# Last pass of a graph network: another row order, five chunks' layers from split parts, shorter split lead

## The reference

```python
def mlp(x, W1, b1, W2, b2, W3, b3):            # a = leaky_relu, slope 0.01
    return a(a(a(x @ W1 + b1) @ W2 + b2) @ W3 + b3)

x = layernorm(x + relu((adj @ x) @ kernel + bias))
u = x
for _ in range(3):
    v = mlp(adj @ u, *uv)
    u = mlp(adj @ v, *vu)                      # the third u is not used
out = layernorm(x + v)
```

## Time and profile before

| | |
|---|---|
| median of three runs | 1168.94 us (1168.66 to 1168.98) |
| the profiled execution | 1168.49 us |
| its span, first to last instruction | 1166.7 us, so 1.8 us lie around it |
| granted TensorE clock | 0.999 of full |
| TensorE busy, its weight loads | 99 %, 82 % |
| VectorE, ScalarE busy | 63 %, 57 % |

### The profile page before, as it was taken

The page is one execution under the profiler, slowest core; times in us unless marked ns, Lnnn a source line. Parts: engine busy times, 40 slices in busy tenths (PEclk is TensorE's granted clock), DMA queues, the critical chain, the costliest instruction groups (busy, mean ns, idle before and its releaser), DMA issues.

```text
span 1166.7 us, 13724 instructions
## 1 busy us (share of the span) xinstructions
PE 1153.5 (99%) x5242; PEld 954.0 (82%) x5242; DVE 736.7 (63%) x888; ACT 659.3 (57%) x811; POOL 4.9 (0%) x10
## 2 busy tenths in 40 slices
PE   7999999999999999999999999999999999999998
PEld 6888888888888888888888888888888888887876
DVE  7997676458555555555545746553566554678985
ACT  7765555346554555555444755553556544667874
POOL 0000000000000000000000000000000000000001
PEclk9999999999999999999999999999999999999999
DMA  9988786568356646555656636655575656579971
GB/s 383 405 301 322 251 270 198 200 216 288 120 205 217 210 157 213 199 195 181 205 188 220 238 124 211 205 179 198 192 242 165 212 186 230 166 292 356 312 281 36
DMA packets 72353, 261.60 MB, mean 224 GB/s; under 512 B 8032, under 2 KB 8800, under 8 KB 71264
## 3 DMA queue, kind: packets, MB, share of 16 engines
q1 hardware_dynamic: 72144, 260.61, 64.0%
q10 hardware_dynamic: 144, 0.13, 0.0%
HBM read 258.61 MB, written 2.10 MB: 223 GB/s over the span
## 4 chain that ended last, share of the span: by engine, by line
PE 94%; DMA 3%; DVE 1%; ACT 0%; SPq 0%; issue 0%; ACTq 0%
PE agg_ps L932 29%; PE agg_ps L925 28%; PE agg_ps L918 28%; PE pre_ps L829 4%; DMA adj_raw<-in_adj 3%; PE hid_ps L790 1%; PE hid_ps L792 1%; PE hid_ps L791 1%; DVE adj_lo L770 1%; PE hid_ps L851 1%; PE hid_ps L865 0%; ACT adj_hi L635 0%; DVE stats L648 0%; PE hid_ps L868 0%; SPq L496 0%
## 5 line engine op out<-in xcount | busy, mean ns | idle before, releaser
L770 DVE TENSOR_TENSOR adj_lo<-adj_raw,adj_hi 128x1024 fp32r<-128x1024 f32 x464 | 547.8, 1219 | 224.9 <-ACT adj_hi L635 219.6
L918 PE MATMUL agg_ps<-adj_hi,feat_hi 128*128 128x512 f32 x1484 | 586.4, 395 | 7.5 <-ACT adj_hi L635 7.5
L925 PE MATMUL agg_ps<-adj_hi,feat_lo 128*128 128x512 f32 x1484 | 579.3, 390 | 0.0
L635 ACT ACTIVATE adj_hi<-adj_raw 128x1024 fp32r<-128x1024 f32 x464 | 467.6, 1051 | 83.3 <-PE agg_ps L932 69.1
L932 PE MATMUL agg_ps<-adj_lo,feat_hi 128*128 128x512 f32 x1484 | 458.8, 390 | 0.2 <-DVE adj_lo L770 0.2
L918 PEld LDWEIGHTS agg_ps<-adj_hi,feat_hi 128*128 128x128 f32 x1484 | 279.6, 188 | 66.0 <-issue 9.4
L925 PEld LDWEIGHTS agg_ps<-adj_hi,feat_lo 128*128 128x128 f32 x1484 | 279.5, 188 | 59.1 <-issue 1.9
L932 PEld LDWEIGHTS agg_ps<-adj_lo,feat_hi 128*128 128x128 f32 x1484 | 278.9, 188 | 59.5 <-DVE adj_lo L770 1.1
L528 ACT ACTIVATE hid<-hid_ps,params 128x512 f32<-128x512 f32 (+2 forms) x82 | 55.1, 672 | 59.6 <-PE hid_ps L792 50.7
L600 ACT ACTIVATE in_hi<-part 128x512 fp32r<-128x512 f32 x24 | 15.2, 634 | 110.3 <-DVE part L759 110.3
L528 ACT ACTIVATE post<-pre 128x512 f32<-128x512 f32 x39 | 24.7, 632 | 88.0 <-DVE pre L737 88.0
(11 more groups left out here) (80 smaller groups left out, 389.8 us busy)
## 6 DMA issues: line engine op xcount, KB each, us to landing
adj_raw<-in_adj SPq DMA_DIRECT2D x472, 512.0 KB, 5.6
adj_raw<-in_adj SPq DMA_DIRECT2D x8, 1024.0 KB, 8.1
resid<-in_x SPq DMA_DIRECT2D x8, 256.0 KB, 8.1
out<-resid SPq DMA_DIRECT2D x7, 256.0 KB, 5.3
params<-in_weights SPq DMA_DIRECT2D x1, 386.0 KB, 5.1
b_row<-in_bias_rows SPq DMA_DIRECT2D x1, 128.0 KB, 5.7
out<-resid SPq DMA_DIRECT2D x2, 64.0 KB, 1.8
out<-resid ACTq DMA_DIRECT2D x1, 128.0 KB, 1.9
```

Of the source, the lines that this page charges most:

```text
L635: act.activation(split_hi(b)[:, i * CHUNK:(i + pieces) * CHUNK], adj_raw[:, h % RAW, 0:pieces * CHUNK], ACT.Copy).then_inc(adj_hi_ready, 1)
L770: dve.tensor_tensor(split_lo(b)[:, slot], adj_raw[:, h % RAW, 0:pieces * CHUNK], split_hi(b)[:, slot].bitcast(F32), ALU.subtract).then_inc ...
L918: pe.matmul(group_bank(g), feat_hi[feats][:, tile(src, i)], split_hi(b)[:, piece(i)], start=start, stop=False)
L925: pe.matmul(group_bank(g), feat_lo[feats][:, tile(src, i)], split_hi(b)[:, piece(i)], start=False, stop=False)
```

## The change

Three things change, all in the last pass. The row order becomes 6, 1, 5, 4, 3, 2 (after 7 and 0). The first five units (rows 0, 7, 6, 1, 5) become `LAST_PARTS`: they are calculated in parts like the units of the passes 1 to 4, with offsets of their own that reach to piece 36 after the row's end. Splits are due 14 pieces ahead, not 20. Row 4 takes the kind `LATE2` and row 3 the kind `LATE`, both with new offsets; the activation of `LATE2` goes to a buffer of its own (a part of `part` that is free by then), so it needn't wait until the unit before it is normalised.

```diff
-LEAD, FIRST_LEAD, LAST_LEAD, FIRST_ROWS = 12, 4, 20, 3
+LEAD, FIRST_LEAD, LAST_LEAD, FIRST_ROWS = 12, 4, 14, 3
...
+    LAST_PARTS: dict(dve_sum=0, act_in=3, dve_in=4, pe_hid1=10, act_hid1=11, dve_hid=13, pe_hid2=20, act_hid2=21,
+                     pe_out=25, dve_pre=25, act_post=28, dve_stats=29, act_std=32, dve_shift=33, act_norm=36),
...
-    LATE3: dict(dve_sum=0, act_in=0, pe_hid1=6, act_hid1=7, pe_hid2=10, act_hid2=11, pe_out=14, dve_pre=14,
-                act_post=16, dve_stats=17, act_std=20, dve_shift=20, act_norm=24),
-    LATE2: dict(dve_sum=0, act_in=1, pe_hid1=4, act_hid1=5, pe_hid2=7, act_hid2=8, pe_out=9, dve_pre=10,
-                act_post=10, dve_stats=12, act_std=14, dve_shift=15, act_norm=16),
-    LATE: dict(dve_sum=0, act_in=1, pe_hid1=1, act_hid1=2, pe_hid2=3, act_hid2=5, pe_out=5, dve_pre=7, act_post=7,
-               dve_front=8, dve_total=8, dve_stats=9, act_std=12, dve_root=13, pool_norm=13),
+    LATE2: dict(dve_sum=0, act_in=0, pe_hid1=5, act_hid1=6, pe_hid2=9, act_hid2=10, pe_out=13, dve_pre=13,
+                act_post=14, dve_stats=15, act_std=18, dve_shift=18, act_norm=22),
+    LATE: dict(dve_sum=0, act_in=1, pe_hid1=3, act_hid1=4, pe_hid2=5, act_hid2=7, pe_out=7, dve_pre=9, act_post=9,
+               dve_front=10, dve_total=10, dve_stats=11, act_std=14, dve_root=15, pool_norm=15),
...
-LAST_ROWS = (6, 5, 4, 3, 1, 2)
+LAST_IN_PARTS = 5
+LAST_ROWS = (6, 1, 5, 4, 3, 2)
...
-                          "act_post": max(ends.get("act_norm", -1) if self.steps_of(u) != END else -1,
+                          "act_post": max(ends.get("act_norm", -1) if self.steps_of(u) not in (LATE2, END) else -1,
...
-                else LATE3 if after == 3 else LAST
+                else LAST_PARTS if u < self.rows * (PASSES - 1) + LAST_IN_PARTS else LAST
...
-        return self.steps_of(u) in (IN_PARTS, TURN)
+        return self.steps_of(u) in (IN_PARTS, TURN, LAST_PARTS)
...
-            if plan.steps_of(u) in (END, END2):
+            if plan.steps_of(u) in (LATE2, END, END2):
                 return part_of(chunk_of(plan.first_of(u) - 1))
...
-                        wait_for_normed(act, u - 1)
+                        if plan.steps_of(u) != LATE2:
+                            wait_for_normed(act, u - 1)
...
-                u = at(t, "dve_hid", HIDDEN)
+                u = at(t, "dve_hid", DEEP)
...
-                u = at(t, "dve_in", HIDDEN)
+                u = at(t, "dve_in", DEEP)
```

More of the change, by code:

```diff
@@ L40 @@
 HOLD = 3
-LEAD, FIRST_LEAD, LAST_LEAD, FIRST_ROWS = 12, 4, 20, 3
+LEAD, FIRST_LEAD, LAST_LEAD, FIRST_ROWS = 12, 4, 14, 3
 LOAD_GCN, LOAD_PARAMS = 24, 90
 W_SPLIT = 320
-IN_PARTS, TURN, LATE3, LATE2, LATE, END, END2 = "in_parts", "turn", "late3", "late2", "late", "end", "end2"
+IN_PARTS, TURN, LAST_PARTS, LATE2, LATE, END, END2 = "in_parts", "turn", "last_parts", "late2", "late", "end", "end2"
 STEPS = {
```

## The result

| | before | changed |
|---|---|---|
| median of five runs | 1168.78 us (1168.54 to 1168.98) | 1175.79 us (1175.39 to 1177.12) |
| profiled execution | 1168.49 us, span 1166.7 | 1175.79 us, span 1174.0 |

The ratio is 1.0062, 95 % interval 1.0048 to 1.0076: slower, by 7.0 us. The lines of the changed file lie one or two further down: 528 and 560 are now 529 and 561, 918, 925, 932 are now 920, 927, 934; 790 is 792, 851 and 865 are 853 and 867, 829 is 831, 770 is 772, 759 is 761, 745 and 750 are 747 and 752, 737 is 739, 635 is 637.

What follows compares the result with a forecast made beforehand. TensorE, 99 % busy, was taken to set the time, with VectorE and ScalarE nearly full in the last pass. -1.8 + 9.2 - 0.2 = +7.2 us on 1168.5 gives 1175.7 profiled, 1176.1 median; range 1168.0 to 1179.0.

Steps and rivals of the forecast that it cites:

- the likeliest case: Last pass: TensorE waits 5 to 10 us for layers, giving 1172 to 1177.5 us; chance 0.62.
- TensorE's saving, 1.8 us: Five units, two layers each: a layer in parts takes 0.68 us, not 0.86, so 1.8 us less TensorE work.
- The added work: Last pass, units in parts: VectorE gets 6.0 us more work, ScalarE 4.4 us more.
- The waits, 9.2 us: TensorE at layers of rows 6, 1, 5 and 3, by a walk of the queues: 9.2 us, 0.26 there already.
- VectorE's idle times in the stretch, 8.1 us in 15: From row 7's dve_hid (piece -89) to row 3's sum (-12): VectorE loses 8.1 us, 14 waits for ScalarE splits.
- The written-out link: Row 1's statistics (-41) to row 5's second layer (-28): VectorE needs 7.2 us, starts 5.0 late, TensorE waits 2.7.
- The lead: Splits due 14 pieces ahead, not 20: doesn't cause the waits; with 20 the walk gives 3 us less.
- The loads: Each load is issued 8 splits, about 10.9 us, ahead of use and lands in 5.6 us: hidden.
- The tail: From piece -9 to the end: as long as before, what follows piece -3 being the same list.
- VectorE keeps up: Rival, last pass: every layer finds its parts, only saved work shows, -1.8 - 0.3, 1166.8 us; chance 0.15.
- Work alone: Rival: VectorE's 65.9 us without holes, only row 3's sum late, about 1168.0; half or no holes, chance 0.15.
- The clock falls: Third rival: TensorE's waits lower its clock, +2.5 us, 1178.6, or loads land late; chance 0.08 for clock or loads.

Runs made afterwards that it cites:

- the plan without waits: Changed kernel, all five units still in parts, with row order 1, 6, 5, 4, 3, 2, lead 17 and other offsets: 1166.25 us, ratio 0.9979 to the kernel before.
- the one with lead 20: Changed kernel with splits due 20 pieces ahead again, all else as changed: 1173.84 us, ratio 1.0041 to the kernel before.
- the later square root: Changed kernel with act_std, dve_shift and act_norm of the units in parts 2 pieces later, same work: 1172.34 us, ratio 1.0036 to the kernel before.
- the lighter ScalarE: Changed kernel normalising only the first of four tiles of a chunk in the five units in parts: 1173.54 us, ratio 1.0038 to the kernel before.
- the one with lead 24: Laid-out plan (row order 1, 6, 5, 4, 3, 2) with lead 24 in place of 17: 1175.36 us, ratio 1.0053 to the kernel before.
- the kernel with row 4's statistics behind the sum: Changed kernel with row 4's dve_stats, act_std and dve_shift 2 pieces later, behind row 3's sum on VectorE: 1173.41 us, ratio 1.0040 to the kernel before.

## Why the prediction was right

It said 1176.1 us and 1175.79 was measured, by the likeliest case and its mechanism. That the profiled execution agrees within 0.1 us (1175.7 was said for it) is partly luck: the waits came out 0.5 us smaller than said, and 0.7 us that the prediction didn't have makes up for them. Nor did the median lie 0.45 us above the profiled execution this time; it is the same. Point by point:

- *TensorE's saving, 1.8 us.* Not seen by itself in the changed kernel, but in the plan without waits: 2.4 us faster by the medians, where 1.8 and the 0.3 us wait of before make 2.1. In the sum of TensorE's work in the stretch two terms are 0.1 us too large (7 x 0.68 is 4.8 and 2 x 0.86 is 1.7), so 66.5 should be 66.3 us; the argument stays.
- *The added work.* VectorE's 6.0 us is what the page shows. Of ScalarE's 4.4 us it shows 3.4, as busy time; what the eight instructions cost in the queue wasn't measured apart.
- *The waits, 9.2 us* (the six that are listed make 9.1). From start to start on TensorE, less the normal distance: row 6's second layer 1.6 (1.5 was said), row 1's output layer 0.2 (0.4), row 5's first layer 1.2 (1.2) and second 2.6 (2.7), its output under 0.1 (0.2), row 3's first layer 3.1 (3.1). Together 8.7, of which 0.3 was there before; less the saved 1.8 that makes 6.6 us. The two traces move apart by 6.9 us in the last pass, so 0.3 has no name; the other 0.4 of the 7.3 us between the two profiled executions is there at the pass's beginning (an output layer at 1044.70, before at 1044.26).
- *VectorE's idle times in the stretch, 8.1 us in 15.* All waits of VectorE from 1083 to 1155 us in the changed kernel:

```profile
DVE adj_lo L772 <- ACT adj_hi L637: 3.7, 8, 0.9
DVE feat_lo L772 <- ACT feat_hi L637: 2.4, 6, 0.6
DVE part L720 <- ACT part L529: 0.7, 1, 0.7
```

  Fifteen, of 6.8 us: 14 for ScalarE's splits and one for row 4's activation, as said. The term was a little too large, as was the lateness: at row 1's statistics 6.0 us where the walk had 6.4. (They start at 1127.55. Their piece lies three pieces, 2.04 us, before the one at which row 5's first layer was due, 1123.11 + 0.45 = 1123.56.) VectorE doesn't once wait for TensorE at 739 there; such a wait was named as the sign of being wrong.
- *The written-out link.* From 1127.55 to the end of `hid_lo` at 1134.78: 7.2 us, with holes of 0.21 and 0.58 where 0.27 and 0.66 were said.
- *The lead.* It was said not to be the cause of the waits, and to give back 3 us at 20. Measured 2.0 by the medians, 3.4 by the profiled executions (the last section is on the difference).
- *The loads.* "Hidden" holds for TensorE, which waits for no split in the last pass. ScalarE did wait for them: seven times, 3.0 us in all, between 1054 and 1067 us, where the kernel before and the one with lead 20 have no such wait. They don't carry into the stretch: VectorE is idle 3.11 us after them, before 1071.87, and with lead 20, without them, the waits at rows 6 and 5 are the same.
- *The tail* is as long: from the last product (853, 256 columns) on both kernels are 7.3 us apart, as at the end.

The rivals. *VectorE keeps up*: it doesn't, at these offsets; the plan without waits shows that it can. The Trainium skill (Perfetto Trace Analysis, Identifying the Most-Contended Engine) says to optimise the engine with the highest occupancy first, over the span TensorE. The work saved there shows in these runs only where TensorE has no wait in the last pass. The section Optimization Strategy of the same page says that the most contended engine can change over time; the windows agree, with VectorE at 44.70 and TensorE at 45.06 of 50 us from 1100 on. *Work alone*: refuted twice, by the later square root and by the lighter ScalarE, 3.4 and 2.3 us less by the medians with VectorE's work unchanged. *The clock falls*: the profiled execution shows 0.999 for the span and 1.00 in each of the windows with waits, but other executions show something of it. The 5 us of slower products in its price stand in no row, and no run shows them.

## What to carry to other kernels

Where one engine is busy all the time and two others feed it from queues in order, the question is not how much work they have over the span but whether their queues, in the stretch at hand, still reset: here a VectorE that waited for TensorE at the output layers had spare time, and one that never did stayed late by the sum of all that came before. An instruction that waits for the other helper stood better behind the work that this one needs next. And before giving up a cheaper form because it came out slower, walk the queues with the durations of the trace: the same instructions cost 7 us in one order of rows and set of offsets and gave 2.4 us in another.

## What was not expected

In kernels whose longest wait in the last pass is 1.9 to 3 us, executions of one kernel can fall into two groups that differ in the mean granted clock. The lead-20 kernel took 1172.4 us twice with a clock of 0.999 over the span, and 1173.8 to 1174.6 three times with 0.997 or 0.998; the kernel with the later square root 1172.1 to 1172.3 three times at 0.999, and 1173.7 to 1173.8 twice at 0.998 and 0.997; with the lighter ScalarE 1172.1 twice at 0.999 and 1.000, and 1173.5 to 1173.9 three times at 0.997. The changed kernel has one of five at 1177.12 us and 0.998 (and another at 0.998 that isn't longer), and the one with lead 24 three of five at 0.998. The kernels with no wait over 1 us beside the one at the start have 0.999 or 1.000 in every execution and spread under 1.5 us. So with waits of this length some executions take 1.3 to 2 us more, at the lower clock. That the wait brings the clock down is likely, but not shown. The profiled executions caught none of these, so which wait it would be isn't shown either; and the kernel with row 4's statistics behind the sum had a wait of 2.4 us and a clock of 1.000 five times out of five. The prediction's third rival had this at 2.5 us, as a case of its own; it comes on top of the main case instead, in part of the executions.
